# Perceiver block on one core: the product of r from rounded and low parts, a fetch without its explicit wait, and new places in the five lists

## The reference, cut to what matters

```python
x = x + xattn(layernorm(x), ctx)      # self attention, cross attention over 2048 rows, two-layer MLP
x = x + rwkv(layernorm(x))            # the block below
x = x + moe_attention(layernorm(x))   # attention whose values and outputs are gated experts
...
xx = xprev - x                        # the time step is the batch row: xprev is 0 for row 0, row 0 for row 1
xr, xw, xk, xv, xa, xg = (x + xx * m for m in (mu_r, mu_w, mu_k, mu_v, mu_a, mu_g))
r = xr @ Wr
w = exp(-exp(-softplus(-(w0 + xw @ Ww)) - 0.5))
k, v = xk @ Wk, xv @ Wv
a, g = sigmoid(a0 + xa @ Wa), sigmoid(xg @ Wg)
...
y = groupnorm(y) * lnx_w + lnx_b + (r_ * k_ * r_k).sum(-1) * v_
att = y * g @ Wo
h = layernorm(x + att) * norm_w + norm_b
out = layernorm(silu(h @ Wf + bf)) * lnf_w + lnf_b
```

## Time and profile before

| | us |
|---|---|
| median of 3 runs (228.45 to 229.44) | 229.01 |
| the profiled execution's own time | 230.31 |
| its span, first to last instruction | 228.60 |
| PE busy in the span | 217.5 |
| DVE busy in the span | 176.1 |
| ACT, POOL busy in the span | 112.9, 102.2 |

### The profile page before, as it was taken

One profiled execution on the slowest core, in us unless ns is written; L12 is line 12 of the kernel. 1 busy time (PEld: TensorE's weight loads), 2 busy tenths in 40 slices (PEclk: granted clock), 3 DMA queues, 4 the chain that ended last, 5 costly groups with the idle time before them and its releaser, 6 DMA issues.

```text
span 228.6 us, 3249 instructions
## 1 busy us (share of the span) xinstructions
PE 217.5 (95%) x1201; PEld 170.9 (75%) x1201; DVE 176.1 (77%) x320; ACT 112.9 (49%) x217; POOL 102.2 (45%) x90
## 2 busy tenths in 40 slices
PE   8999999999999999999889999989969899999995
PEld 7898899789888888879475657454547669798963
DVE  2155982878598987997689894999966899898971
ACT  2356532473689588755134488898211221246210
POOL 5025005660667446986510139896936117170000
PEclk9999999999999999999999999999997999999999
DMA  6999998079983699358762305000690000000002
GB/s 236 429 419 419 452 429 367 13 282 422 307 331 132 244 429 383 139 184 368 265 288 57 130 0 184 0 0 1 236 422 33 0 0 3 0 1 3 0 12 80
DMA packets 6783, 43.99 MB, mean 192 GB/s; under 512 B 880, under 2 KB 1392, under 8 KB 2032
## 3 DMA queue, kind: packets, MB, share of 16 engines
q1 hardware_dynamic: 6624, 43.66, 48.1%
q10 hardware_dynamic: 144, 0.13, 0.2%
HBM read 43.27 MB, written 0.52 MB: 192 GB/s over the span
## 4 chain that ended last, share of the span: by engine, by line
PE 79%; DMA 9%; DVE 6%; issue 2%; ACT 2%; POOL 1%; SPq 0%; DVEq 0%; POOLq 0%
PE psum L424 61%; PE psum L466 13%; DMA ring<-blocks 4%; DMA bc<-vecs 3%; PE psum L428 3%; ACT slots L1600 2%; DVE small L907 1%; DMA slots<-xin 1%; DVE slots L917 1%; PE psum L440 1%; PE psum L600 1%; POOL small L1923 1%; DVE slots L913 1%; DVE slots L929 1%; SPq L351 0%
## 5 line engine op out<-in xcount | busy, mean ns | idle before, releaser
L424 PE MATMUL psum<-ring_r,slots_r 128*128 128x512 f32 x360 | 90.2, 404 | 0.8 <-DVE slots_r L1105 0.4
L424 PEld LDWEIGHTS psum<-ring_r,slots_r 128*128 128x128 f32 x360 | 67.3, 191 | 19.7 <-ACT slots_r L1600 2.9
L1928 POOL TENSOR_TENSOR ring_r<-ring,ring_r 128x640 fp32r<-128x640 f32 x21 | 43.5, 2082 | 27.5 <-ACT ring_r L1600 27.4
L1600 ACT ACTIVATE slots<-psum 128x256 f32<-128x256 f32 (+4 forms) x48 | 20.3, 451 | 61.4 <-PE psum L424 24.0
L1600 ACT ACTIVATE ring_r<-ring 128x2048 fp32r<-128x2048 f32 x23 | 43.8, 1913 | 10.8 <-PE psum L424 8.9
L424 PE MATMUL psum<-ring,slots 128*128 128x512 f32 (+5 forms) x122 | 41.5, 483 | 2.1 <-issue 1.0
L935 DVE TENSOR_TENSOR ring_r<-ring,ring_r 128x1408 fp32r<-128x1408 f32 x21 | 35.8, 1706 | 3.3 <-ACT ring_r L1600 3.3
L466 PE MATMUL psum<-slots,ring 128*128 128x128 f32 x320 | 37.5, 276 | 0.3 <-ACT slots L1600 0.3
L466 PEld LDWEIGHTS psum<-slots,ring 128*128 128x128 f32 x320 | 36.5, 192 | 0.9 <-ACT slots L1600 0.7
L424 PEld LDWEIGHTS psum<-ring,slots 128*128 128x128 f32 (+1 forms) x122 | 19.9, 190 | 17.2 <-issue 13.9
L1923 POOL TENSOR_TENSOR small<-small,mhalf 128x1 f32<-128x1 f32 x16 | 8.8, 549 | 47.2 <-DVE small L909 45.9
(11 more groups left out here) (179 smaller groups left out, 255.0 us busy)
## 6 DMA issues: line engine op xcount, KB each, us to landing
ring<-blocks SPq DMA_DIRECT2D x36, 1024.0 KB, 7.7
bc<-vecs SPq DMA_DIRECT2D x1, 3072.0 KB, 16.5
bc<-vecs SPq DMA_DIRECT2D x2, 512.0 KB, 15.6
bc<-vecs SPq DMA_DIRECT2D x1, 768.0 KB, 7.6
slots<-xin SPq DMA_DIRECT2D x1, 256.0 KB, 5.1
y<-slots SPq DMA_DIRECT2D x1, 256.0 KB, 2.1
y<-slots SPq DMA_DIRECT2D x2, 128.0 KB, 1.8
slots<-xin ACTq DMA_DIRECT2D x1, 128.0 KB, 2.8
```

Of the source, the lines that this page charges most:

```text
L424: return t.matmul(o_, l, r, start=first, stop=last)
L1600: return a.activation(o, x, func, **kw)
L1928: g.tensor_tensor(ring_r[:, p, CUT:], ring[:, p, CUT:], ring_r[:, high(name), CUT:], ALU.subtract).then_inc(*split_lowg.inc(name))
```

## The change

`r` joins the products that are made in parts (`STEPS`), for both rows: its weights are split by ACT, DVE and POOL into place 12, its rows into rounded and low parts. To make room, `ro` and `rf` take other places for their rounded weights. The fetch of `fk` no longer has an explicit wait on the products of `g` and moves ahead; `bc2` now stands behind a wait on the products of `v`. All five lists get a new order in many places; no other computation is added or removed. The core of the diff, in the order SP, PE, ACT, DVE, POOL:

```diff
-PARTED = {"v1": 12, "v2": 12, "ro": 12, "rf": 10, "rk": 10, "ra": 11, "rv": 9}
-STEPS = "kav"
+PARTED = {"v1": 12, "v2": 12, "ro": 10, "rf": 11, "rk": 10, "ra": 11, "rv": 9, "rr": 12}
+STEPS = "kavr"
...
             fetch("rk")
+            fetch("rr")
             fetch("ra")
-            fetch("rg")
+            fetch("f1")
             fetch("rv")
             fetch("f2")
+            fetch("fk")
+            fetch("fo")
             fetch("ro")
+            fetch("rg")
             fetch("rw")
-            fetch("rr")
-            fetch("fo")
+            fetch("fg")
             fetch("rf")
             for b in range(2):
-                s.wait_ge(*prod[b].at("g"))
-            fetch("fk")
+                s.wait_ge(*prod[b].at("v"))
+            fetch("fq")
             s.wait_ge(*normed[0].at("n4"))
             s.wait_ge(*normed[1].at("n4"))
             eng.dma_start(bc[:, 2:len(BCAST) - FIRST_BC, :], spread(FIRST_BC + 2, len(BCAST))).then_inc(s_bc2, 16)
-            for b in range(2):
-                s.wait_ge(*prod[b].at("v"))
-            fetch("fq")
-            fetch("fg")
...
+            f1(1)
+            f2(1)
+            turned_rows(0, "n4", N4[0], 0)
...
             bias("a0", 1)
-            f1(1)
-            turned_rows(0, "n4", N4[0], 0)
-            f2(1)
+            step(0, "a", 0, 1, bias_of="a0")
             step(0, "k", 1, 2)
...
             turned_rows(1, "n4", N4[1], 4)
+            step(0, "v", 2, 3, wait=normed[0].at("x3"))
+            step(1, "k", 0, 5, wait=evict[1].at("relu"))
...
             step(0, "r", 3, 0, wait=turned[0].at("n4"))
-            step(1, "k", 0, 5, wait=evict[1].at("relu"))
...
+            lift(0)
             step(0, "g", 4, 1, wait=rk_v[0].at("c"))
-            lift(0)
             step(1, "g", 5, 6, wait=rk_v[1].at("km"))
...
+            split_weight("rr", prod[0].at("v2"), prod[1].at("v2"))
...
+            round_step("r", 3)
...
+            low("rr")
...
+            low_step0("r", 3)
...
+            low_step1("r", 3)
...
+            low("rr")
...
-            mixr = MIX[1][1].rearrange("p (c n) -> p c n", c=4)
+            mixr = PART[1][1]
```

More of the change, by code:

```diff
@@ L842, in _ @@
             lift(1)
+            s.wait_ge(*rk_v[1].at("ys"))
+            s.wait_ge(*rk_v[1].at("c3"))
+            s.wait_ge(*rk_v[1].at("c1"))
+            bias("bf", 4)
             ro(0)
@@ L1358, in _ @@
             nonzero(0, 0)
+            low("ct11")
+            nonzero(0, 2)
             nonzero(0, 1)
@@ L1402, in _ @@
             low("ra")
+            low("rk")
+            low("rv")
             low_pc(1)
-            weigh2(1)
-            low_row("a0")
             add2(1)
@@ L1414, in _ @@
             start4(0)
+            low("rr")
             norm(0, "n4", N4[0], X[0])
-            low("rk")
-            low_row("lnx_b")
-            low_step0("k", 1)
-            low_step0("a", 0)
             add3(1)
@@ L1422, in _ @@
             norm3(1)
+            low_step0("a", 0)
             done3(1)
             start4(1)
+            low_step0("k", 1)
             norm(1, "n4", N4[1], X[1])
-            low("rv")
+            low_row("lnx_b")
+            low_step0("v", 2)
             s.wait_ge(*turned[0].at("n4"))
@@ L1431, in _ @@
             mix("k", 0)
-            low_step0("v", 2)
+            mix("a", 1)
             low_step1("k", 0)
-            mix("a", 1)
+            low_step0("r", 3)
+            low_step1("a", 1)
+            low_row("bf")
+            centre_v(0)
             keys_c(0)
             keys(0)
-            low_step1("a", 1)
             read_keys(0)
@@ L1441, in _ @@
             v.tensor_reduce(keep["rn"], heads(sc_[1]), AX.X, ALU.add).then_inc(*own_v.inc())
-            centre_v(0)
-            keys_c(1)
-            s.wait_ge(*rk_g[1].at("c2"))
-            v.tensor_reduce(keep["c2"], heads(c2t), AX.X, ALU.add).then_inc(*own_v.inc())
-            keys(1)
+            s.wait_ge(*own_v.now())
+            v.tensor_scalar(keep["rn"], keep["rn"], 1e-24, None, ALU.max).then_inc(*own_v.inc())
             s.wait_ge(*sq_a[0].at("vc"))
@@ L1500, in _ @@
                                    op1=ALU.mult).then_inc(*rk_v[0].inc("yg"))
-            s.wait_ge(*rk_v[1].at("ss"))
+            s.wait_ge(*own_v.now())
+            v.tensor_tensor(keep["al"], keep["c1"], keep["c2"], ALU.subtract).then_inc(*own_v.inc())
             s.wait_ge(*own_v.now())
@@ L1504, in _ @@
             s.wait_ge(*own_v.now())
-            v.tensor_tensor(keep["m11"], keep["m11"], ss[1], ALU.mult).then_inc(*own_v.inc())
+            v.tensor_tensor(heads(ys[1]), heads(vc[0]), over(keep["al"], 64), ALU.mult).then_inc(*own_v.inc())
+            s.wait_ge(*own_v.now())
+            v.scalar_tensor_tensor(out=keep["m01"], in0=keep["m01"], scalar=2.0 / 64, in1=ss[1], op0=ALU.mult,
+                                   op1=ALU.mult).then_inc(*own_v.inc())
+            s.wait_ge(*own_v.now())
+            v.tensor_tensor(ssq[1], keep["m00"], keep["al"], ALU.mult).then_inc(*own_v.inc())
             s.wait_ge(*own_v.now())
@@ L1514, in _ @@
             s.wait_ge(*own_v.now())
-            v.tensor_tensor(heads(ys[1]), heads(vc[0]), over(keep["al"], 64), ALU.mult).then_inc(*own_v.inc())
-            s.wait_ge(*own_v.now())
             s.wait_ge(*by_a[1].at("sc"))
@@ L1864, in _ @@
             act(TMP[0], vc[0], ACT.Square, scale=0.125).then_inc(*sq_a[0].inc("vc"))
-            split_weight("rf", prod[0].at("k"), prod[1].at("k"))
+            mix1("r", 3)
+            tanh(1, "a", "th", th_p[1], 6)
+            s.wait_ge(*evict[1].at("th"))
+            act(th[1], th_p[1], ACT.Copy, scale=0.5, bias=0.5).then_inc(*sq_a[1].inc("a"))
+            round_step("r", 3)
             s.wait_ge(*const.at("wbias"))
@@ L1996, in _ @@
             mul(X[1], X[1], vec("ln3_b"), x_off[1], "x3", ALU.add)
[L1997 to L2000 removed]
+            low("c13")
+            deviation(0, "x2")
+            low("rv")
+            low("rk")
             s.wait_ge(*normed[0].at("x2"))
@@ L2039, in _ @@
             mul(rs8[0], rs8[0], ss[0], rk_g[0], "rs")
+            s.wait_ge(*rk_v[1].at("ys"))
+            s.wait_ge(*rk_v[1].at("rn"))
+            mul(sc_[1], ys[1], vec("r_k"), rk_g[1], "sb")
+            low_third("ro", 1)
+            s.wait_ge(*rk_v[1].at("vc"))
+            s.wait_ge(*rk_v[1].at("c2s"))
+            mul(c2t, vc[0], vc[1], rk_g[1], "cov")
             s.wait_ge(*mixed[1].at("g"))
```

417 lines of the change are left out of this document (197 added, 220 removed), and 4 rows, old and new, of the table prod.

## The result

| | before | after |
|---|---|---|
| median of 17 runs each, us | 229.01 (227.54 to 231.69) | 227.42 (226.99 to 228.23) |
| ratio to before | 1 | 0.9936 [0.9914, 0.9957] |
| profiled execution, us (span) | 230.31 (228.6) | 227.37 (225.6) |
| granted clock, mean of the profiled span | 0.993 | 1.000 |

The change gains 1.6 us in the medians. (The ratio, which gives 1.5, leaves out one run of before, 231.69, that lies more than 1.5% above the fastest.) The forecast was 225.1, so 2.3 us of the forecast gain of 3.9 are missing. The two profiled executions are 2.94 apart, nearly twice as much as the medians; that is the first hint at what went wrong.

What follows compares the result with a forecast made beforehand. PE was taken to bound the kernel until about 99 us, then a chain of waits through DVE and a transfer. -2.1 (h turned earlier) and -1.8 (clock) make -3.9: 225.1 us against the median; 8-in-10 range 223.0 to 228.8.

Steps and rivals of the forecast that it cites:

- `rf` runs at 1.00: 4.55 - 2.74 = -1.8: First rf on PE: with the hole before h smaller, the clock stays at 1.00, saving 1.8 us.
- 229.01 - 2.1: Turning of h of row 0 on PE: forecast at 168.5 instead of 170.63, 2.1 us earlier.
- What is late next: POOL's root ... about 0.2: Before h of row 0: once the vectors come early, POOL's root for h is the next wait, about 0.2 us.
- weighed a rule and put it aside: DVE beside POOL: SBUF exclusion would make the sum 0.4 us higher; the prediction went by profile rows and added nothing.
- The row that was set against the rule, 1.27 on POOL: A POOL product of 1.27 us, where DVE hardly pauses, taken to show that nothing is added.
- where rr is split (0.4): Subtractions of rr on DVE and POOL: under the exclusion rule, the product of a would wait some 0.4 us.
- Before the MLP: +0.5 forecast: 0 to 103 us: a later second exponential of row 1 (0.4) and turn_pc (0.1) cost PE 0.5 us.
- The MLP's holes of 0.84 and 0.97: PE's waits before f2 and before n4 of row 0 go; new waits on ACT total 0.55, net -1.26 us.
- The hole before g of row 1: Middle block on PE: a new wait of 1.6 us for POOL's mixg, bounds 0 and 2.9.
- PE's -1.1 to the end of g of row 1: PE from the start through g of row 1: its terms sum to 1.1 us earlier.
- The end of the list, 164.5 forecast: DVE's list from 119 us: 0.9 more work, 1.6 less idle, so yg of row 1 ends 0.7 us earlier.
- the clock falls anyway: Rival for rf, chance 0.24: other holes still bring the clock down, only -2.1 stays, giving 226.9 us.

Runs made afterwards that it cites:

- run 12: Run 9's kernel with fq's 1 MB fetch also ahead of the three vectors: 232.80 us, ratio 1.0114, a clock fall in 5 of 6 runs.
- run 1: The kernel before, unchanged, measured against itself: 228.99 us, ratio 0.9994; 4 of 12 runs show the clock fall.
- Run 4: The changed kernel with POOL's last third of rf's low part and additions of lnf_b moved away from the affines of h: 226.05 us, ratio 0.9867.
- run 10: Run 7's kernel with ACT rounding v's rows earlier, and POOL's third of ro and product for a behind DVE's low parts: 226.39 us, ratio 0.9888.
- run 5: The changed kernel with POOL's mixing of g's rows put two places earlier: 227.20 us, ratio 0.9935.
- 2: The kernel before with only the fetch of the three vectors issued earlier, behind the wait on v: 226.90 us, ratio 0.9895.
- 9: Run 4's kernel with the end of SP's list as before the change (fk, then vectors, behind g; then fq): 227.61 us, ratio 0.9916.
- 8: Run 7's kernel with r's product plain again: 226.75 us.
- 7: The changed kernel with both changes of POOL's list, those of run 4 and run 5: 226.15 us, ratio 0.9891.
- 6: The changed kernel with r's product plain again, all places and orders kept: 227.58 us, ratio 0.9954.
- 3: The changed kernel with the fetch of the vectors put back behind the waits on g of both rows: 227.26 us.

## Why the prediction was wrong

The direction was right, and the measured time lies in the range. The size failed in two steps, 1.3 + 1.0 = 2.3 us.

**The step that failed: the clock, and the base it was taken from.** The step says "`rf` runs at 1.00: 4.55 - 2.74 = -1.8", and the sum then takes all 3.9 off the median. Its mechanism holds: with the hole down to 0.91 no run of after shows the fall, and a longer hole brings it (run 12). Its size holds in a run that has the fall: 4.62 against 3.02 in the timelines, and 1.6 between the two groups of before's runs. But the fall is in 38 of 86 runs, and of its 1.6 only 0.5 stand in the median (229.21 against 228.69): the term of 1.8 was 1.3 too large for the base it was taken from. The prediction had the sign in hand: the profiled execution lay 1.3 above the median. From the profile's own base the sum gave 226.4, and against 227.37 in the profile of after 1.0 is missing; from the median it gave 225.1, and 2.3 is missing. A fall that costs 1.6 to 1.8, in a profile 1.3 above the median, should have been charged to the profile first: 229.01 - 2.1 = 226.9. With the 0.5 that the runs now show it is 226.4, and the 1.0 below makes 227.4 of it.

**The other 1.0: "What is late next: POOL's root ... about 0.2".** What is late next is the affine itself, 1.95 for 0.75. Against run 1's trace: `yg(1)` is 0.61 earlier (164.66 to 164.05; 0.7 in the prediction), the wait of 1.55 is gone, the affine costs 1.20 more. That makes -0.96 for the turning of `h(0)`; measured is 169.65 - 170.71 = -1.06. Run 4 takes POOL away and turns `h(0)` at 168.36, against the forecast 168.5; its 226.05 lies 0.35 under the 226.4. This is the place where the prediction weighed a rule and put it aside. The Trainium skill, SBUF — State Buffer, section "Who interferes with whom", says that a DVE instruction with two SBUF inputs and a POOL instruction that reads SBUF exclude each other, and that one that only writes does not. The traces agree where POOL works on hundreds of columns: 1.95 beside POOL's subtraction, 0.75 without it and beside memsets, and 0.69 for line 1188, which has one operand in PSUM, wholly beside POOL's addition of 168.99 (0.70 with POOL idle, before). They don't where POOL's instruction is the `pow` of run 10, which reads 8 columns and did not hold DVE during its 1.65. The row that was set against the rule, 1.27 on POOL, proved nothing: DVE's instructions beside it were sums with one input and a product with one operand in PSUM. The trace of before had a row that speaks for the rule: line 923, the affine, also runs at 99.52, beside a subtraction of POOL, and takes 1.80 there. The two rows of before, first DVE's, then POOL's:

```profile
99.52 1.80 DVE L923 SCALAR_TENSOR_TENSOR slots<-slots,small,bc 128x512 f32<-128x512 f32 x1
```

```profile
99.20 1.57 POOL L1928 TENSOR_TENSOR ring_r<-ring,ring_r 128x640 fp32r<-128x640 f32 x1
```

The prediction's other row, POOL's 21 subtractions that average 2.08, is a mean of 1.53 to 3.03. And the rule was weighed only where rr is split (0.4), not where the new order puts POOL's reads beside the affine.

**The rest, point by point.** Before the MLP: +0.5 forecast; `x2(0)` is turned at 102.45 instead of 101.50, +0.95. The MLP's holes of 0.84 and 0.97 went; PE waits 0.26 and 0.57 for ACT where 0.2 and 0.35 were forecast, and 0.49 for k of row 1 where 0.85 was. r: 24 matmuls (r and v) in 5.69, 2.85 for twelve, as forecast. The hole before g of row 1: 1.6 forecast, 1.39 measured. PE's -1.1 to the end of g of row 1 is -0.54 (160.24 against 160.78 in run 1). As the prediction said, neither decides: run 5 takes the hole away and gains nothing, since DVE's list sets `yg(1)`. The end of the list, 164.5 forecast and 164.74 measured, is right in part by luck: from 119 us to there DVE is busy 42.73 in after, 2.0 more than in run 1's trace where the walk had 0.9, and idle 2.6 less where it had 1.6. Rows that lengthened beside POOL are in the surplus, which the walk left out, such as this one beside the subtractions of rr and ra (DVE and POOL of after; the other five executions of line 911 take about 0.55):

```profile
119.64 1.79 DVE L911 TENSOR_SCALAR slots<-slots,small 128x512 f32<-128x512 f32 x1 [0.44 <-POOL small L1927]
```

```profile
119.61 3.22 POOL L1932 TENSOR_TENSOR ring_r<-ring,ring_r 128x640 fp32r<-128x640 f32 x2
```

It has only one SBUF input of 512 columns; that POOL held it is read off these two rows, no run tries it apart. Behind `h(0)`'s turning 56.39 became 55.95, within the half us allowed. Of the rivals, "the clock falls anyway" (226.9) has the nearest number, but by luck: the clock doesn't fall anyway, in most runs it didn't fall before.

What the change consists of, in medians: the vectors without `fk` ahead of them, 1.1 to 1.8 (runs 2 and 9); the parts of r, 0.6 where nothing hides them (8 against 7), and not resolved in the changed kernel itself (6); POOL at the affine, 1.0 to 1.2 given back (4 against 3, 7 against 5). The fall that it spares some runs adds about 0.5 to the median. These are differences between several kernels, and their sum isn't measured as one.

## What to carry to other kernels

Look at where one profiled execution lies among the runs before taking a term out of it: a fall of the clock that is visible in a profile above the median belongs to that profile, and only a part of it to the median. When POOL's work moves, go down DVE's list beside it and mark each instruction with two SBUF operands: each can grow by what is left of POOL's instruction, and the profile shows it as a longer duration and not as a wait. Then look in the trace for the same line at two durations, as line 923 before (0.75 and 1.80): it shows what can be held before anything is changed. Line 911 (0.55 and 1.79 in after) suggests that one wide SBUF operand may be enough. An engine's hole that another engine's full list sets is worth nothing: follow the wait that ends last before filling it.

## What the runs showed of the hardware

- The same program falls to the lower clock in some executions and not in others: 38 of 86, in two groups of mean clock (0.990 to 0.993, and 0.997 to 1.000) with medians of 230.30 and 228.69. A hole of 3.95 us brought the fall in 5 of 6.
- Small instructions are held as well: a product of 128x8 on DVE went from 0.16 to 0.84 beside a POOL product of 1.29. An edit that brought DVE forward by about 0.5 lost it all to this.
- POOL's `pow` of 128x8 didn't hold DVE: two subtractions of 128x512 with two SBUF inputs took 0.69 each beside it (run 10).
- The same transfer of 768 KB lands 4.0 or 5.0 us after its issue with no fetch issued just ahead of it (runs 2 and 3), after 6.2 to 7.6 behind one of 1 MB (after, before, runs 4 and 9), and after 9.5 behind two (run 12).
